# A layer norm emitted one step earlier in a sigmoid-attention phase, and its squares moved from GpSimd to ScalarE

## The reference

```python
x = x + attn_a(layernorm(x))     # chunked linear attention, 8 heads
x = x + ffn(layernorm(x))        # gelu(x @ w1 + b1) @ w2 + b2, 1024 -> 4096 -> 1024
x = x + attn_b(layernorm(x))
x = x + ffn(layernorm(x))

def attn_b(x):                   # N = 4096, D = 1024
    Q, K, V = (sigmoid(4 * (bn(x @ W) - 1)) for W in (Wq, Wk, Wv))
    t_Q = 1 - Q.mean(-1, keepdims=True);  t_K = 1 - K.mean(-1, keepdims=True)
    dt = t_Q - swapaxes(t_K, 1, 2)
    f = 0.9 * exp(-abs(dt) / 0.5)
    A = where(dt < 0, f, -f) + 0.9
    return A @ V @ Wo + bo
```

## Time and profile before

| | us |
|---|---|
| median of 3 runs | 5795.34 |
| lowest, highest | 5790.23, 6011.71 |
| the profiled execution | 5788.37 |
| its spans, cores 0 to 7 | 5767.8 to 5786.7 |
| its slowest core (3) | 5786.7 |

### The profile page before, as it was taken

The page is one execution under the profiler, slowest core; times in us unless marked ns, Lnnn a source line. Parts: engine busy times, 40 slices in busy tenths (PEclk is TensorE's granted clock), DMA queues, the critical chain, the costliest instruction groups (busy, mean ns, idle before and its releaser), DMA issues.

```text
span 5786.7 us, 75332 instructions; the slowest of 8 cores (5767.8 to 5786.7 us)
## 1 busy us (share of the span) xinstructions
PE 4000.4 (69%) x26176; PEld 2477.8 (43%) x26176; DVE 1996.2 (34%) x4078; ACT 1339.5 (23%) x2420; POOL 251.4 (4%) x228
## 2 busy tenths in 40 slices
PE   1666677673888888966677666455454468888889
PEld 0333333332666666832222222111111156666678
DVE  3555555553222222221112112554555522222221
ACT  0111111111222222211222113333333222222222
POOL 0000000000000000011111210000000000000000
PEclk7777877776999999979888899999999879999999
DMA  4233222224000000030000000000010140000000
GB/s 139 74 95 95 95 95 95 95 81 160 30 30 30 30 30 30 16 117 15 15 15 15 29 0 1 30 29 30 31 57 29 37 139 30 30 30 30 30 23 23
DMA packets 111995, 290.35 MB, mean 50 GB/s; under 512 B 6930, under 2 KB 72722, under 8 KB 101394
## 3 DMA queue, kind: packets, MB, share of 16 engines
q1 hardware_dynamic: 111634, 285.54, 14.7%
HBM read 193.25 MB, written 92.27 MB: 49 GB/s over the span
## 4 chain that ended last, share of the span: by engine, by line
PE 55%; DVE 22%; ACT 10%; issue 6%; DMA 3%; POOL 1%; DVEq 1%; ACTq 0%; SPq 0%; POOLq 0%
PE PS L247 49%; DVE BIG L1058 3%; ACT BIG L1054 3%; DVE BIG L1060 3%; ACT BIG L1051 3%; PE PS L914 3%; PE PS L387 2%; DVE BIG L1048 2%; ACT BIG L907 2%; PE PS L391 1%; DVE LNB L767 1%; DVE LNB L763 1%; DVE LNB L769 1%; DVE LNB L473 1%; DVEq L146 1%
## 5 line engine op out<-in xcount | busy, mean ns | idle before, releaser
L247 PE MATMUL PS<-BIG,AB 128*128 128x256 bf16 (+2 forms) x10496 | 1480.3, 299 | 639.4 <-DVE BIG L1060 499.2
L247 PE MATMUL PS<-LNB,AA 128*128 128x256 bf16 (+1 forms) x10176 | 1399.5, 296 | 287.7 <-POOL LNB L473 96.2
L247 PEld LDWEIGHTS PS<-BIG,AB 128*128 128x128 bf16 x10496 | 1030.0, 100 | 1071.8 <-issue 801.7
L247 PEld LDWEIGHTS PS<-LNB,AA 128*128 128x128 bf16 x10176 | 933.8, 98 | 758.7 <-issue 382.2
L823 ACT ACTIVATE BIG<-PS,B1C 128x256 bf16<-128x256 f32 x1024 | 485.9, 475 | 1329.1 <-PE PS L247 1328.3
L387 PE MATMUL PS<-LNB,CON 128*128 128x256 bf16 (+1 forms) x360 | 150.8, 419 | 449.1 <-DVE LNB L372 448.7
L763 DVE CAST LNB<-XB 128x256 bf16<-128x256 f32 x256 | 72.2, 292 | 933.8 <-PE PS L247 914.0
L247 PE MATMUL PS<-AB,AA 128*128 128x512 bf16 x1088 | 282.3, 419 | 134.9 <-DVE XB L724 83.5
L1058 DVE SCALAR_TENSOR_TENSOR BIG<-SQ,SKC,BIG 128x512 f32<-128x512 f32 x256 | 192.3, 751 | 440.5 <-ACT BIG L1054 440.5
L842 DVE SCALAR_TENSOR_TENSOR XB<-PS,B2C,XB 128x256 f32<-128x256 f32 x256 | 123.6, 483 | 589.1 <-PE PS L247 585.9
L1051 ACT ACTIVATE BIG<-BIG 128x512 f32<-128x512 f32 x256 | 161.3, 630 | 656.1 <-DVE BIG L1048 656.1
(11 more groups left out here) (111 smaller groups left out, 2729.5 us busy)
## 6 DMA issues: line engine op xcount, KB each, us to landing
AB<-w SPq DMA_DIRECT2D x64, 512.0 KB, 4.4
xBbuf<-XB SPq DMA_DIRECT2D x16, 2048.0 KB, 7.2
XB<-xBbuf SPq DMA_DIRECT2D x32, 1024.0 KB, 5.0
XB<-xCbuf SPq DMA_DIRECT2D x16, 2048.0 KB, 11.1
XB<-xT SPq DMA_DIRECT2D x8, 2048.0 KB, 8.0
AA<-wcA SPq DMA_DIRECT2D x16, 1024.0 KB, 6.6
AB<-wcB SPq DMA_DIRECT2D x16, 1024.0 KB, 6.4
xCbuf<-XB SPq DMA_DIRECT2D x16, 1024.0 KB, 4.4
```

Source lines behind the costliest of these rows:

```text
L247: inst = t.matmul(oap if oap is not None else psum_ap, lh, rh, start=st, stop=sp)
```

## The change

`ln_pass` squares on ACT in every case. And in rounds 0 to 5 `bload_ln(s + 1)` is emitted whole, ahead of `v_proj(s)`, with `vw_mm(s)` after `v_proj(s)`. Round 6 keeps the order of before (the LN of slice 7 writes LNB, which `v_proj(6)` still reads), and round 7 has no next slice.

```diff
-            if alt_scratch:
-                P.op("p", (lambda p, d=x2, so=xa: p.tensor_tensor(
-                    d, so, so, ALU.mult)),
-                     reads=xregs,
-                     writes=(x2r,) + (tuple(extra_war) if c == 0 else ()))
-            else:
-                P.op("s", (lambda s_, d=x2, so=xa: s_.activation(d, so, AF.Square)),
-                     reads=xregs,
-                     writes=(x2r,) + (tuple(extra_war) if c == 0 else ()))
+            P.op("s", (lambda s_, d=x2, so=xa: s_.activation(d, so, AF.Square)),
+                 reads=xregs, writes=(x2r,) + (tuple(extra_war) if c == 0 else ()))
@@
             qk_sums(s)
-            v_proj(s)
-            if s + 1 < nsl:
+            if s + 2 < nsl:
+                bload_ln(s + 1)
+                v_proj(s)
+                vw_mm(s)
+            elif s + 1 < nsl:
+                v_proj(s)
                 bload_ln(s + 1, mid=lambda s2=s: vw_mm(s2))
             else:
+                v_proj(s)
                 vw_mm(s)
```

## The result

The changed kernel is slower, by 1.2%: the ratio to the kernel before is 1.0116, with a 95% interval of 1.0087 to 1.0146. Its profiled execution took 5864.59 us, against 5788.37 before and 5861 predicted.

The account below looks back on a forecast made before the run. TensorE and its standstills bound the kernel; a round grows from 54.9 to 69.0 us, less 2.2 saved in Q and K; six rounds give +71.4, with round 6 +73: 5861 us, range 5840 to 5888, to 5900 with table loads.

Parts of the forecast that it names:

- The chain of LN(s+1): From complete statistics through DVE's rsqrt arithmetic and the DVE and POOL apply: 30.5 us, unchanged by the change.
- two groups: v_proj matmul groups PE can run before both PSUM banks wait for sigmoid 0: 3.5 us cover instead of 14.0.
- The step on which the sign hung: v_proj's first sigmoid waits by name for LN(s+1)'s apply: six PE idle stretches of some 24 to 28 us.
- The terms of the round: T0 to next Q matmul: statistics 10.0, chain 30.5, sigmoid 0.9, six v_proj groups 12.5, wait 1.1, vw_mm 14.0; 69.0 us.
- The Q and K section: Q and K sums after vw_mm lose their slow start: 2.2 us saved a round, up to 2.7.
- The six rounds: Rounds 0 to 5, each net +11.9 us: +71.4 us together.
- the lost early square: ACT makes the first square later than POOL did: 0.2 us in rounds 0 to 5, 1.5 us once in round 6.
- The estimate of 32 us: Twelve ACT table switches between Square and Sigmoid, with drain: 5893 us; the table-load rival had chance 0.07.
- The rival of a lasting low clock: All 48 v_proj matmuls behind the wait run at 1.2 GHz: +53 us, 5914 us; chance 0.05.
- The rival that the cover works: Sigmoid not held by LN(s+1), so matmuls cover the chain: 40.5 us a round, 5694 us; chance 0.04.

Follow-up runs that it names:

- e1: The changed kernel with the five LN scratch names removed from the writes of v_proj's first sigmoid; ratio 0.9835 to the kernel before, profiled 5695.94 us.
- e5: The changed kernel with v_proj's first sigmoid keeping only lnm2 of the five LN scratch names; ratio 0.9936 to the kernel before, profiled 5757.87 us.
- e3b: The kernel before with only the new order in rounds 0 to 5, squares left on POOL; no ratio (spread), profiled 5865.84 us.
- e4: The kernel before, old order, with the five LN scratch names removed from v_proj's first sigmoid; no ratio (spread), profiled 5791.51 us.
- e2: The kernel before with only the squares moved to ACT, order untouched; no ratio (spread), lowest time 5790.62 us.
- e6: The changed kernel with the whole LN apply on DVE instead of split with POOL; ratio 1.0135 to the kernel before, profiled 5851.76 us.

## Why the prediction was right, point by point

- *The bound.* The chain of LN(s+1) (30.5 us) was 30.5 us again: L388 at 2650.79, POOL's end at 2681.28. Its cover fell from vw_mm to two groups, as was said.
- *The names.* The step on which the sign hung, `_collect` on the five names, is shown by e1 and e5, and that the order brings it out by e3b and e4.
- *The terms of the round.* In round 0 the statistics took 10.45 (10.0 taken, 8.8 to 11.0 as bounds), the chain 30.5, the sigmoid 1.0 (0.9), then 13.78 from the third group to vw_mm (2682.30 to 2696.08; 12.5 and 1.1 taken), vw_mm 13.8. Together 69.5, against 69.0.
- *The Q and K section* took 66.96 us in round 1, where the earlier trace rows had 67.80: 0.8 saved, where 2.2 was taken. Over all six rounds and eight cores, in medians, it went from 68.8 to 66.1 us, 2.7 saved, and T0 to Q from 54.8 to 70.1 (54.9 and 69.0 taken). So the sum of the round was 1.1 us too low and the saving 0.5 too low, and the two errors partly cancel.
- *The six rounds* cost +73.3 us in the slowest cores and +76.0 in the medians; +71.4 was predicted. From core to core they take 738.0 to 743.8 us in the kernel before and 814.5 to 818.5 in the changed one.
- *The squares.* The prediction named 0.2 us a round for the lost early square and left it out of its sum; e3b against the changed kernel gives 0.6. In round 6 it took 1.5 us; there the statistics went from 8.76 us (3401.59 to 3410.35) to 9.88 (3473.80 to 3483.68), +1.1. At the start of the phase the change gained something that the prediction missed: from the first cast to the first Q matmul it took 42.2 to 42.6 us before and 41.4 to 41.5 after, in all cores. No table load came. The estimate of 32 us that the prediction worked out from the figures of the Trainium skill ("ScalarE: Activation LUTs", What ACT_TABLE_LOAD costs) would need a switch between sets, and there was none: the page's rule isn't contradicted, its condition wasn't met.
- *The clock.* The 27.21 us wait had four microseconds at 0.51 behind it, no more than the 16.64 and 30.25 us waits before. The rival of a lasting low clock fell. The one thing that was not said clearly: the statistics ran at the low level from their third matmul on, at a granted clock of 0.57. The sum had them between the two levels, 0.45 us below what was measured.
- *Luck in it.* The start of round 0 and the phases ahead vary by some 10 us between executions; an error of 3 us in 5861 is better than the sum deserves.

The rival that the cover works was priced at 5694 us. It was wrong for this change and right for e1, which took 5695.94.

## What to carry to other kernels

When an operation is emitted earlier, look at every name that the operations behind it write, and not only at what they touch: a wait list that was satisfied long ago can become the longest wait of the loop. Price a move by its new cover (what can really run behind the wait, bank by bank), and then price it once more with the list cleaned; here the same move took the profiled execution from 5788 to 5865 or to 5696 us. Operations that only gate a DMA, like the memset here, belong ahead of the work on their engine.

## What the runs showed of the hardware that was not expected

- PE fell to the low clock (1.2 GHz) in a stretch in which it was never idle for more than 0.7 us at a time: 16 matmuls in 10.45 us, granted clock 0.57. In the kernel before the same sixteen matmuls, behind a dense v_proj, ran at 1.00 (2658.60 to 2667.45). Ahead of the slow stretch stood the Q and K sums with their 1.2 us waits. e2 has the squares on ACT too, but the statistics behind v_proj, and there each matmul took 0.38 us and a chunk 1.16 us (2662.24 to 2663.40 on core 4); so it is the place of the statistics, and not the squares, that brings the low clock. That it is the work ahead which decides is argued from these stretches. The price is 1.37 against 1.17 us a chunk.
- Giving POOL half of the apply made the chain longer, not shorter: 16.6 us against 12.8 on DVE alone (16 x 0.797). POOL takes 1.26 and 1.16 us where DVE takes 0.69. But a name has its part in this too: POOL's first multiply stands idle for 5.46 us until DVE's last one, since both write the name of the LN buffer. Without this wait the split chain would take some 11.1 us (16.6 less 5.5, an estimate from these rows), less than on DVE alone; no run tried it. POOL's first subtract (1.77) and DVE's multiply beside it (1.56 instead of 0.69) seem to slow each other: in e6, with POOL idle, DVE's first multiply took 0.69 as well.
